# A second halving add on GpSimd ahead of VectorE's softmax row sum, in a fused cross-attention and quantised feed-forward kernel

## The reference

```python
x = x + xattn(layernorm(x), ctx, Wq, Wkv_expand, Wout)     # ctx: 8 x 64 x 64, 16 heads of width 16
x = x + ffn(layernorm(x), w1, g1, w2, g2, w3, g3)          # hidden width 1024

# xattn
scores = einsum('bhqd,bhkd->bhqk', qh, kh) * inv_sqrt_d    # 256 queries x 64 keys per head, causal
attn = softmax(where(tril, scores, min), axis=-1)
out = einsum('bhqk,bhkd->bhqd', attn, vh) @ Wout.T
# ffn
linear_bit(x, w, g) = act_quant(rmsnorm(x, g)) @ ternary_quant(w).T
h = silu(linear_bit(x, w1, g1)) * linear_bit(x, w2, g2);  return linear_bit(h, w3, g3)
```

## Time and profile before

| | us |
|---|---|
| median of 3 runs (lowest to highest) | 215.14 (214.61 to 218.46) |
| span of the profiled execution | 215.0 |
| VectorE busy in it | 184.2 |
| TensorE matmuls busy in it | 170.9 |
| ScalarE busy in it | 152.4 |
| GpSimd busy in it | 143.6 |

### The profile page before, as it was taken

How to read it: one execution, slowest core, us unless ns; L and a number is a source line. 1 busy time by engine, 2 the same in 40 slices (tenths; PEclk the granted TensorE clock), 3 DMA queues, 4 the chain that set the end, 5 groups by cost and what they waited for, 6 DMA issues and landing times.

```text
span 215.0 us, 3666 instructions
## 1 busy us (share of the span) xinstructions
PE 170.9 (79%) x1073; PEld 110.0 (51%) x1080; DVE 184.2 (86%) x338; ACT 152.4 (71%) x218; POOL 143.6 (67%) x229
## 2 busy tenths in 40 slices
PE   4799877998997998999948878447489978788372
PEld 4755545585674865747436545124236544454251
DVE  2359799599999899997995889799999999999981
ACT  2355888958665896859864998829499968877622
POOL 5216292555667696886461666879899999999640
PEclk9999999999999999999997999959969999999979
DMA  6999000000000000000000000000000100010011
GB/s 163 340 377 361 27 3 2 0 2 5 0 0 3 0 0 0 0 0 3 2 0 0 0 3 0 0 2 0 30 24 24 49 24 24 24 52 24 24 49 49
DMA packets 8798, 9.09 MB, mean 42 GB/s; under 512 B 1488, under 2 KB 8400, under 8 KB 8784
## 3 DMA queue, kind: packets, MB, share of 16 engines
q1 hardware_dynamic: 8512, 8.65, 12.4%
q10 hardware_dynamic: 272, 0.26, 0.4%
HBM read 6.82 MB, written 2.10 MB: 41 GB/s over the span
## 4 chain that ended last, share of the span: by engine, by line
DVE 38%; issue 21%; PE 16%; ACT 12%; POOL 10%; DMA 2%; DVEq 1%; POOLq 0%; ACTq 0%
DVE hh L1195 5%; DVE probs L948 4%; DVE c_max L1213 4%; ACT q_x L819 4%; POOL u L384 4%; PE bank L555 3%; PE wide L511 3%; DVE m_x L1066 3%; DVE u_max L1059 3%; PE bank L706 2%; POOL half_sum L366 2%; DVE row_sum L955 2%; ACT hT L880 2%; DVE row_max L942 2%; PE bank L494 2%
## 5 line engine op out<-in xcount | busy, mean ns | idle before, releaser
L687 PE MATMUL wide<-wT,xqT 128*128 128x512 bf16 x128 | 33.5, 406 | 5.7 <-DVE hh L1195 3.5
L404 POOL TENSOR_TENSOR c_h<-hh,g3b 128x1024 f32<-128x1024 f32 x15 | 35.4, 2361 | 2.9 <-DVE hh L1195 2.5
L511 PE MATMUL wide<-k_diag,qT 128*128 128x512 f32 x64 | 28.9, 595 | 0.3 <-DVE k_diag L1000 0.3
L875 ACT ACTIVATE sq_junk<-hh,root_x 128x1024 bf16<-128x1024 f32 x16 | 18.4, 1147 | 15.2 <-DVE hh L1195 15.2
L706 PE MATMUL bank<-wT,hT 128*128 128x256 bf16 x128 | 17.6, 283 | 11.8 <-ACT hT L880 11.8
L334 POOL TENSOR_TENSOR k_diag<-kT,head_of 128x512 f32<-128x512 f32 x15 | 15.4, 1045 | 12.6 <-DVE kT L996 7.3
L819 ACT ACTIVATE q_x<-u,round_c,qs_x 128x256 f32<-128x256 f32 x32 | 16.6, 590 | 9.4 <-issue 5.1
L384 POOL TENSOR_TENSOR u<-xc,g 128x512 f32<-128x512 f32 x16 | 20.3, 1290 | 4.4 <-ACT q_x L819 4.4
L687 PEld LDWEIGHTS wide<-wT,xqT 128*128 128x128 bf16 (+1 forms) x128 | 12.3, 102 | 20.6 <-issue 7.3
L366 POOL TENSOR_TENSOR half_sum<-probs 128x512 f32<-128x512 f32 x16 | 20.1, 1277 | 3.4 <-ACT probs L779 3.3
L706 PEld LDWEIGHTS bank<-wT,hT 128*128 128x128 bf16 x128 | 11.6, 100 | 20.5 <-ACT hT L880 16.8
(11 more groups left out here) (139 smaller groups left out, 385.8 us busy)
## 6 DMA issues: line engine op xcount, KB each, us to landing
w_in<-in_L_ffn_w SPq DMA_DIRECT2D x3, 1024.0 KB, 10.3
out<-y SPq DMA_DIRECT2D x16, 128.0 KB, 1.7
x_sb<-in_x SPq DMA_DIRECT2D x1, 1280.0 KB, 12.4
x_sb<-in_x SPq DMA_DIRECT2D x1, 512.0 KB, 5.3
g3b<-in_L_ffn_g SPq DMA_DIRECT2D x1, 512.0 KB, 7.9
wq_in<-in_L_xattn_Wq ACTq DMA_DIRECT2D x1, 256.0 KB, 4.0
x_sb<-in_x SPq DMA_DIRECT2D x1, 256.0 KB, 3.6
wout_in<-in_L_xattn_Wout SPq DMA_DIRECT2D x1, 256.0 KB, 12.2
```

The source lines that it names most:

```text
L404: g.tensor_tensor(out=c_h[:, t, :], in0=hh[:, t, :], in1=g3b[:], op=ALU.mult).then_inc(c_ready, 1)
L511: last = nc.tensor.matmul(wide[:, n * 512:(n + 1) * 512], qT[:, c, t * P:(t + 1) * P], k_diag[:, c, :, :], start=(t == 1), stop=True)
L687: last = nc.tensor.matmul(wide[:, (w * 2 + n) * 512:(w * 2 + n + 1) * 512], xqT_cols(T, w * DC + c), w_cols[:, 4 * n:4 * n + 4, c, :], sta ...
```

## The change

GpSimd's two halving adds now each signal `half_ready`. GpSimd waits for both, and one further instruction adds the upper 16 of the 32 half sums of every row to the lower 16, in place, for both tiles at once (128 x 512 elements in each operand and in the output); it signals the new semaphore `quarter_ready`. VectorE waits for that, and its row sum reads 16 elements a row, in runs of 16 with gaps of 16 (128 x 512 in).

```diff
@@ half_sums(b), GpSimd
                     for t in range(TB):
                         need(pool, probs_ready, 2 * b + t + 1)
                         e = probs[:, t, :].rearrange("p (n h k) -> p n h k", h=2, k=SK // 2)
-                        last = g.tensor_tensor(out=half_sum[:, t, :, :], in0=e[:, :, 0, :], in1=e[:, :, 1, :],
-                                               op=ALU.add)
-                    last.then_inc(half_ready, 1)
+                        g.tensor_tensor(out=half_sum[:, t, :, :], in0=e[:, :, 0, :], in1=e[:, :, 1, :],
+                                        op=ALU.add).then_inc(half_ready, 1)
+                    need(pool, half_ready, 2 * b + 2)
+                    g.tensor_tensor(out=half_sum[:, :, :, 0:SK // 4], in0=half_sum[:, :, :, 0:SK // 4],
+                                    in1=half_sum[:, :, :, SK // 4:SK // 2], op=ALU.add).then_inc(quarter_ready, 1)
@@ sums(b), VectorE
-                    need(dve, half_ready, b + 1)
-                    v.tensor_reduce(out=row_sum[:], in_=half_sum[:], op=ALU.add, axis=AX.X).then_inc(sums_ready, 1)
+                    need(dve, quarter_ready, b + 1)
+                    v.tensor_reduce(out=row_sum[:], in_=half_sum[:, :, :, 0:SK // 4], op=ALU.add, axis=AX.X).then_inc(sums_ready, 1)
```

More of the change, by code:

```diff
@@ L146, in build_program @@
             "scores_done", "max_ready", "shifted", "probs_ready", "sums_ready", "recip_ready"))
-        recip_wide, kp0_ready, half_ready = sem("recip_wide"), sem("kp0_ready"), sem("half_ready")
+        recip_wide, kp0_ready, half_ready, quarter_ready = sem("recip_wide"), sem("kp0_ready"), sem("half_ready"), sem("quarter_ready")
         pT_done, pT_ready, pv_done, rT_done, rT_ready, attnT_ready = map(sem, (
```

## The result

The changed kernel takes 223.28 us (median of 4 runs, 222.78 to 224.24), against 214.88 us for the kernel before on the same occasion. The ratio is 1.041, 95% interval 1.037 to 1.044: slower by 4%. The forecast was slower, 221.0 us within 217 to 225.

What follows compares the result with a forecast made beforehand. VectorE was taken to bound the attention period (busy 12.27 of 12.69 us). Eight batch terms, 0.82 + 0.82 + 0.23 + 0.98 + 1.14 + 0.61 + 0.62 + 0.71 = 5.93 us, on a 215.0 us span gave 221.0 us, range 217.0 to 225.0.

Steps and rivals of the forecast that it cites:

- I let the second `xc` go first: Batch 2: second `xc` starts just ahead of the new add, which runs 54.69 to 55.96; row sum 0.76 late, net +0.23 us.
- What is queued behind it: GpSimd's `factor`, `keys` and `norm` start up to 1.35 us later behind the new add; costed at nothing.
- my signs: Trace signs listed for a right forecast, among them VectorE waiting for `half_sum` before the row sums of batches 0 to 2.
- a later `qs_x` moves that residual in full: Batches 3 and 4: `qs_x` delay passes through ScalarE and TensorE to the residual; costs 0.98 and 1.14 us.
- I let L1071 meet the new add: Batches 4 and 5: L1071 stalls until the new add ends, +1.14 us each, batch 5 net +0.61.
- Hidden: Rival: new add stalls nothing on VectorE, only direct waits count; +1.0, 216.1 us; chance 0.13.
- VectorE first: Rival, batches 4 to 6: VectorE's chain runs ahead of the add, row sum waits; 220.7 us; within the main case's 0.60.
- Partly absorbed: Rival: existing waits or shifted timing make two or three seams cost nothing; 217.5 to 219.4 us; chance 0.12.
- TensorE slows down too: Rival: one to three more slow projections, 1.7 us each; 222.7 to 226 us; chance 0.13 shared with no reduce saving.

Runs made afterwards that it cites:

- the unread add: Kernel before with the added GpSimd add written to a tile nobody reads, VectorE's row sum unchanged: 223.19 us, ratio 1.031.
- the kernel without adds: Kernel before with GpSimd's half adds removed and VectorE reducing all 64 probabilities of a row: 216.49 us, ratio 1.002.
- the kernel with these two alone: Changed kernel with the added add and shorter row sum in batches 0 and 1 only: 219.59 us, ratio 1.013.
- the changed kernel again: The changed kernel run and profiled once more, nothing altered, against the kernel before: 222.35 us, ratio 1.027.
- two unread adds: Kernel before with two equal added GpSimd adds, no wait between them, into a tile nobody reads: 230.82 us, ratio 1.072.
- the one-tile kernel: Kernel before with GpSimd's half add for a batch's first tile only, VectorE reducing the second from `probs`: 215.75 us, ratio 1.000.

## Why the prediction was right, and where it was off

The mechanism was as forecast. The stalls are shown by the unread add, by two of them and by the kernel without adds; the waits of batches 0 and 1 by the kernel with these two alone.

**Sizes: right.** Row sum 0.69 us (measured 0.686), new add 1.27 (1.28), the gap ahead of it 0.08 (70.56 to 70.64).

**The seams.** How late each row sum starts against the kernel before, the 1.0 us at the start of the execution taken off:

| batch | forecast | profile after | the changed kernel again |
|---|---|---|---|
| 0 | 1.35 | 1.35 | 1.35 |
| 1 | 2.17 | 2.16 | 2.19 |
| 2 | 2.40 | 2.46 | 2.49 |
| 3 | 2.85 | 2.88 | 2.92 |
| 4 | 3.99 | 3.42 | 3.46 |
| 5 | 4.60 | 3.94 | 4.00 |
| 6 | 5.75 | 4.92 | 5.00 |
| 7 | 5.93 | 5.45 | 4.85 |

The forecast column is the running sum of its terms, without what the batch's own shorter row sum gives back behind it. Up to batch 3 it holds within 0.1 us. The two profiles part at batch 7: the projection ahead of it took 3.78 us in the first and 3.26 in the second (before 3.58), and the granted clock stood at its lower level (0.50) for about 7 us there in the first and for 3 to 4 us in the second.

**Batch 2: the total right by luck, two terms wrong.** I let the second `xc` go first; the new add went first, and the pair took 2.77 and not 1.67 us, 1.10 us more. Against it came 0.26 us from iteration 1, where `w_tern` no longer meets `k_diag` (1.22 us, before 1.48), because GpSimd's queue behind the add had moved; that is the term "What is queued behind it", which I had put at nothing. So VectorE did not wait for `half_sum` in batch 2, as my signs had it; the stalled pair covered the add.

**Batch 3: one step failed, "a later `qs_x` moves that residual in full".** The projection came 2.49 us late (L557 at 75.59, less 1.0, against 72.11), `qs_x` 2.88 us. In the kernel before TensorE was still at other transposes when the last `q_x` was done (71.44 us), and went on without a wait; in the changed kernel it stood idle 0.39 us for `q_x`, until 75.36. So 0.39 us of the stall were free. The cover I had not looked for was on the engine in between., one period further on, hints at it: TensorE's matmuls are busy 12.05 of 12.69 us, and 0.86 of VectorE's 12.27 us are the held `m_x` of 92.84, so the period is less VectorE's alone than I read. For batches 4 and 5 the residual did move in full (3.42 and 3.93 us).

**Batches 4 to 6: the stalls over-sized by 0.1 to 0.2 us.** I let L1071 meet the new add. It got through in both hardware-loop iterations, 0.13 us each, though it starts 0.02 us behind the new add by the records (84.54 against 84.52), and the `xc` pair was held: 0.91 us more and not 1.14. In batch 5 the same 0.91 us came with 0.39 us less for the `m_x` ahead (0.63 us, before 1.02), 0.52 in all against 0.61. For batch 6 0.99 and not 1.15, for batch 7 0.71, as forecast.

**Behind the attention.** The forecast let the 5.9 us pass unchanged to the end. In the profiled pair 6.4 us at the last row sum, 1.0 of them of the start, became 8.0 in the feed-forward and 7.5 at the end. VectorE waited 1.5 us for an up-projection at 171.38:

```profile
171.38 1.22 DVE L1197 TENSOR_TENSOR hh<-gate,wide 128x1024 f32<-128x1024 f32 x1 [1.53 <-PE wide L689]
```

The table by stretches has the granted clock there at 0.66, the mean of a part at its upper level (1.00) and a part at its lower (0.50). It gives busy us of each engine, then clock, DMA share and GB/s:

```profile
166.40:171.40 5.00, 4.58 (x30) 3.38 (x31) 2.91 (x7) 3.94 (x6) 4.37 (x8) 0.66 0.07 26
```

In the kernel before a stretch at 0.66 lay at 155 to 160, with VectorE busy 4.93 of 5.00 us, so it cost next to nothing. TensorE had been idle 2.34 us for `hT` just before. The second profile of the changed kernel had no such wait. It was 5.2 us late at the last `hh`, and 7.2 at the end, with the clock at 0.50 from 211.5 us on. With the unread add the 5.4 us at the last row sum were still 5.3 at the last `hh`. So up to 2.4 us come on top of the seams, and they differ with the place of TensorE's slow stretches. That the change causes such stretches is not shown: executions of the changed kernel had a mean clock of 0.93 to 0.96 in all eight runs shown, of the kernel before 0.93 to 0.98.

**The frame of the sum.** I set span and time equal. The span is 1.7 to 1.8 us below the time in every run where both are known. By that the profiled execution of 215.0 us took about 216.7, 1.6 us more than the median run of 215.14. That 215.0 and 215.14 agree is luck and no reason to set them equal. With these 1.6 us, the 1.0 us at the start and the 1.1 us behind the attention, less the 0.5 us that the seams fell short, the forecast of 221.0 becomes 224.2, the time of the profiled execution (224.24). How the median of 223.28 is made up was not traced further. As to the seams alone, the 4.9 to 5.5 us that they cost are 0.5 to 1 us less than the 5.9 forecast.

**The rivals.** "Hidden" falls by the kernel with the unread add; the 4.6 us of stalls named under it would be 4.9 by the prediction's own terms (5.93 less 1.0), which changes no chance. "VectorE first" was right for single instructions and, as worked out, made little difference. "Partly absorbed" was right in kind (0.39 us in batch 3) and too large in size. "TensorE slows down too" did not come as laid out: of the projections only that of iteration 6 is slow (3.78 and 3.26 us), and it was before (3.58). The slow stretches that cost something lay behind the attention.

## What to carry to other kernels

An instruction that is moved to GpSimd may be hidden by every wait in the profile and still cost most of its length (up to 1.1 of 1.28 us here), because VectorE's short instructions with SBUF inputs stand still beside it. Before moving work, lay the two timelines side by side at the place where the new instruction will run, and look which kinds of VectorE instruction fall there: in these traces reduces and statistics pass, `tensor_tensor` of two SBUF tiles, `tensor_scalar` and copies of SBUF do not. Then look what else moves: in three of the kernels here stalls that were saved came back beside another GpSimd instruction (`v_pair` or `k_diag`). A VectorE instruction of four elements that takes 1 us is the sign; VectorE's busy share then counts standing still as work.

## What the runs showed of the hardware

- Beside a GpSimd add (reads and writes SBUF) both a `tensor_tensor` with two SBUF inputs (1.11 us, else 0.16) and a `tensor_scalar` (1.17 us, else 0.13) are held; beside a memset (writes only) the first passes (0.16) and the second is held (0.41 us in batch 3, 0.81 in batches 4 and 5). A copy of four SBUF elements was held beside an add too (1.15 us, else 0.13, with two unread adds).
- With the memset right behind the half adds, a `tensor_scalar` held by a half add stayed held through the memset too, in batches 2 and 6 (2.05 us for four elements in the latter). With an add right behind an add a held `xc` was let through between them (55.16 to 56.60 us in the kernel with two unread adds, the adds meeting at 56.4). Why the two differ is open.
- `tensor_reduce` was never held: `u_max` takes 1.21 us beside a half add, and the eight full row sums of the kernel without adds take 2.269 to 2.286 us. Nor were the statistics (0.42 us for 128 x 256 elements beside a half add).
- Reading runs of 16 elements with gaps of 16 costs the reduce nothing (0.686 us for 512, against 0.68 us for 512 elements without gaps in the one-tile kernel).
- Two profiled executions of one kernel differed by 1.0 us before the first row sum: in one, an input landed 0.31 us later and a group of four transposes on TensorE took 1.00 us, in the other 0.60, and everything behind them moved.
